# Edge columns of the first graph layer, transposed two chunks at a time and read from half of the array's rows

## The reference, cut to what matters

```
def _rgcn_layer(x, src, dst, edge_type, edge_attr, W, root, bias, nn_w, nn_b):
    edge_w = edge_attr @ nn_w.T + nn_b          # 50000 x 32 by 32 x 256
    msg = relu(x[src] * edge_w)
    out = x @ root + bias
    for r in range(3):
        m = where((edge_type == r)[:, None], msg, 0.0)
        s = segment_sum(m, dst)
        cnt = segment_sum(mask, dst)
        out = out + (s / max(cnt, 1)) @ W[r]
    return out
h = x
for l in range(3):                              # three passes, own W, root, bias; same nn_w, nn_b
    h = _rgcn_layer(h, ..., W[l], root[l], bias[l], nn_w, nn_b)
```

## Time and profile before

| | |
|---|---|
| median of three runs | 4751.31 us |
| span of the profiled execution | 4744.9 us (the page has no other time of it) |
| TensorE matmul busy | 3915.0 us, 83% |
| TensorE weight load busy | 3233.3 us, 68% |
| VectorE busy | 3382.7 us, 71% |
| ScalarE busy | 1791.0 us, 38% |
| GpSimd busy | 3071.7 us, 65% |
| DMA | 643 MB, 136 GB/s on average |

### The profile page before, as it was taken

The page is one execution under the profiler, slowest core; times in us unless marked ns, Lnnn a source line. Parts: engine busy times, 40 slices in busy tenths (PEclk is TensorE's granted clock), DMA queues, the critical chain, the costliest instruction groups (busy, mean ns, idle before and its releaser), DMA issues. The chain is left out here.

```text
span 4744.9 us, 105920 instructions
## 1 busy us (share of the span) xinstructions
PE 3915.0 (83%) x22300; PEld 3233.3 (68%) x22301; DVE 3382.7 (71%) x9318; ACT 1791.0 (38%) x5399; POOL 3071.7 (65%) x3178
## 2 busy tenths in 40 slices
PE   6799997889987889878899566779978778578886
PEld 3477775778776778767777556668866666366664
DVE  7799997667757778677787667874257778756666
ACT  0355553221123333333333100004257667367774
POOL 0266665777756777567775777766777773067774
PEclk9799998999998999989999777888978898778787
DMA  1233334856626445264452687861465444144445
GB/s 47 92 131 131 130 132 130 212 126 158 152 63 202 135 145 154 71 185 146 145 149 78 208 257 214 245 191 54 145 182 120 105 106 125 32 99 109 109 109 100
DMA packets 643665, 643.00 MB, mean 136 GB/s; under 512 B 314342, under 2 KB 549540, under 8 KB 643396
## 3 DMA queue, kind: packets, MB, share of 16 engines
q0 software_dynamic: 145840, 374.54, 27.8%
q1 hardware_dynamic: 443348, 213.36, 17.0%
q10 hardware_dynamic: 54336, 53.65, 3.3%
HBM read 470.09 MB, written 170.26 MB: 135 GB/s over the span
## 5 line engine op out<-in xcount | busy, mean ns | idle before, releaser
L1059 POOL DMA_INDIRECT G<-h_dram,idx x1572 | 1525.8, 971 | 556.8 <-issue 361.6
L1283 PEld LDWEIGHTS ps_a<-hotm,msg 128*128 128x128 f32 x4716 | 686.5, 193 | 196.2 <-DVE arena L1395 67.5
L1283 PE MATMUL ps_a<-hotm,msg 128*128 128x128 f32 x4716 | 730.0, 282 | 88.5 <-DVE arena L1395 87.8
L1271 PE MATMUL ps_e<-nnw,attT 128*128 128x256 f32 x2358 | 738.4, 396 | 76.8 <-DVE prodm L1388 42.4
L1395 DVE TENSOR_TENSOR arena<-ps_a,arena 128x256 f32 x1404 | 586.9, 418 | 218.8 <-issue 94.1
L735 POOL DMA_INDIRECT rec_dram<-rec,pos x392 | 376.7, 961 | 398.6 <-ACT rec L606 307.7
L1059 POOL DMA_INDIRECT G<-feat_dram,idx x420 | 402.4, 958 | 325.5 <-POOLq L241 197.9
L1317 ACT ACTIVATE msg<-prodm 128x256 f32<-128x256 f32 x786 | 327.5, 417 | 677.8 <-DVE prodm L1388 586.1
L749 POOL DMA_INDIRECT rec_dram<-rows,place x392 | 379.8, 969 | 222.1 <-issue 117.4
L1897 POOL DMA_INDIRECT arena<-rel_dram,idx x393 | 385.0, 980 | 128.6 <-issue 86.2
L1271 PEld LDWEIGHTS ps_e<-nnw,attT 128*128 128x128 f32 x2358 | 370.3, 195 | 118.4 <-DVE prodm L1388 56.4
(11 more groups left out here) (365 smaller groups left out, 7691.6 us busy)
## 6 DMA issues: line engine op xcount, KB each, us to landing
gate<-rec_dram SPq DMA_DIRECT2D x126, 384.0 KB
G<-msg_dram SPq DMA_DIRECT2D x300, 128.0 KB, 2.2
msg_dram<-msg ACTq DMA_DIRECT2D x270, 128.0 KB
rel_dram<-stage SPq DMA_DIRECT2D x25, 1040.0 KB
G<-h_dram,idx POOLq DMA_INDIRECT x1572
aT<-edge_attr SPq DMA_DIRECT2D x98, 128.0 KB
msg_dram<-arena ACTq DMA_DIRECT2D x90, 128.0 KB
attT<-attT_dram SPq DMA_DIRECT2D x74, 144.0 KB
```

The source lines that it names most:

```text
L1059: pool.indirect_dma_start(G[:, n % width, :], None, table, bass.IndirectOffsetOnAxis(ap=idx[:, which, n:n + 1], axis=0)).then_inc(sem(f"sw ...
L1271: t.matmul(ps_e[s % BANKS][:], attT[:, s // HU, s % HU, :], nnw[:], start=True, stop=True).then_inc(sem("ew"), 1)
L1283: last = t.matmul(ps_a[s % BANKS][:, h, :], of[:, h * P:(h + 1) * P], hot[:, s, :], start=True, stop=True)
```

## The change

- Layer 0 loads edge rows into `att` with 64 columns per chunk. Column 32 is set to one and columns 33 to 63 to zero once.
- TensorE transposes two chunks, 128 columns, at once; the first chunk lands in rows 0 to 63 and the second in rows 64 to 127 of `ps_t`, and one ScalarE copy of 128 x 128 takes both to `attT[:, s // 2]`. A late turn's thirteenth chunk goes alone.
- The edge matmul takes its weights and its `nnw` from 33 rows: 0 to 32 for the first chunk of a pair, 64 to 96 for the second. `nnw` is in both halves. In layer 0 the edge matmul follows the transpose by two steps in place of one.
- `attT_dram` has 128 partitions in place of 32, and a turn's two pieces are 10 and 8 chunks in place of 9 and 9.
- `begin_rgcn` is gone; the four DMAs of `nnw` stand in the kernel's first block.
- In layer 0 the cast for the first turn comes first, and one memset of the whole `arena` follows.
- Bucket numbers are loaded for 18 chunks at once, once a turn, in the three layers and in the gated one.

```
+HALF = P // 2
+PIECES1 = ((0, HU + 1), (HU + 1, U))
-    attT_d = dram("attT_dram", (A32, NC1, P))
+    attT_d = dram("attT_dram", (P, TURNS1 * HU, P))
...
+                        for lo in (0, HALF):
+                            sp.dma_start(nnw[lo:lo + A32, :], L0_gnn_nn_w).then_inc(sem("nnw_in"), 16)
+                            sp.dma_start(nnw[lo + A32:lo + A32 + 1, :], L0_gnn_nn_b.rearrange("(a d) -> a d", a=1)).then_inc(sem("nnw_in"), 16)
...
-                begin_rgcn(nnw, attT)
...
+        def ends_pair(c):
+            return c and not c.extra and (c[2] % 2 == 1 or c.late and c[2] == FRONT - 1)
+        def pair_size(c):
+            return c[2] % 2 + 1
...
-                        att = sb(pctx, "att", [P, U, A32]) if l == 0 else None
+                        att = sb(pctx, "att", [P, U, HALF]) if l == 0 else None
-                        ps_t = ps(pctx, "ps_t", [A32, 2, P]) if l == 0 else None
+                        ps_t = ps(pctx, "ps_t", [P, P]) if l == 0 else None
...
-                                    sp.dma_start(attT[0:A32, h, 0:count, :], attT_d[:, ds(first, count), :]).then_inc(sem(f"att_in{h}"), 16)
+                                    sp.dma_start(attT[:, pairs, :], attT_d[:, ds(i * HU + lo // 2, -(-hi // 2) - lo // 2), :]).then_inc(
+                                        sem(f"att_in{h}"), 16)
...
-                                for c0, c1, c7 in walk(nc.tensor, TURNS1, 0, 1, 7, seams=(SEAM,), late=True):
+                                for c0, c1, c7 in walk(nc.tensor, TURNS1, 0, 2 if l == 0 else 1, 7, seams=(SEAM,), late=True):
...
-                                    if c0 and not c0.extra and l == 0:
+                                    if ends_pair(c0) and l == 0:
                                         n, i, s = c0
-                                        if s % QU == 0:
-                                            pe.wait_ge(sem(f"att_in{s // QU}"), (i + 1) * 16)
-                                        pe.wait_ge(sem("attT_sb"), upto(earlier(c0, 1)))
-                                        t.transpose(ps_t[:, s % 2, :], att[:, s, :], ident[:]).then_inc(sem("attT"), 1)
+                                        for q in range((s - pair_size(c0)) // QU + 1, s // QU + 1):
+                                            pe.wait_ge(sem(f"att_in{q}"), (i + 1) * 16)
+                                        pe.wait_ge(sem("atts_set"), 1)
+                                        pe.wait_ge(sem("attT_sb"), upto(c0.m - pair_size(c0)))
+                                        t.transpose(ps_t[:], att[:, s - s % 2:s - s % 2 + 2, :].rearrange("p s w -> p (s w)"),
+                                                    ident[:]).then_inc(sem("attT"), pair_size(c0))
...
-                                        t.matmul(ps_e[s % BANKS][:], attT[:, s // HU, s % HU, :], nnw[:], start=True, stop=True).then_inc(sem("ew"), 1)
+                                        rows = slice(s % 2 * HALF, s % 2 * HALF + A32 + 1)
+                                        t.matmul(ps_e[s % BANKS][:], attT[rows, s // 2, :], nnw[rows, :], start=True, stop=True).then_inc(sem("ew"), 1)
...
-                                            nc.scalar.copy(attT[0:A32, s // HU, s % HU, :], ps_t[:, s % 2, :]).then_inc(sem("attT_sb"), 1)
+                                        nc.scalar.copy(attT[:, s // 2, :], ps_t[:]).then_inc(sem("attT_sb"), pair_size(c0))
...
                                 if l == 0:
-                                    half = KD * D // 2
-                                    v.memset(arena[:, 0:half], 0.0).then_inc(sem("zeroed"), 1)
+                                    v.memset(att[:, :, A32:A32 + 1], 1.0)
+                                    v.memset(att[:, :, A32 + 1:HALF], 0.0).then_inc(sem("atts_set"), 1)
                                     dve.wait_ge(sem("meta_in"), 16)
                                     v.tensor_copy(idx[:, 0, 0:U], meta[:, 0:U, 1]).then_inc(sem("columns"), 1)
-                                    v.memset(arena[:, half:KD * D], 0.0).then_inc(sem("zeroed"), 1)
-                                    dve.wait_ge(sem("zeroed"), 2)
...
+                                v.memset(arena[:], 0.0).then_inc(sem("zeroed"), 1)
...
-                                bucket = Buckets(nc, mybir.EngineType.DVE, bmap[0:1, 0, :], KD - 1, 8, part=HU)
+                                bucket = Buckets(nc, mybir.EngineType.DVE, bmap[0:1, 0, :], KD - 1, 8, part=U)
...
-                            bucket = Buckets(nc, mybir.EngineType.DVE, bmap[0:1, 1, :], T - 1, 8, part=HU)
+                            bucket = Buckets(nc, mybir.EngineType.DVE, bmap[0:1, 1, :], T - 1, 8, part=U)
```

More of the change, by code:

```diff
@@ L761, in build @@
         meta2 = arena[:, meta2_at:meta2_at + NC2 * REC2].rearrange("p (n w) -> p n w", n=NC2)
[L764 to L780, removed]
         def empty_pads(sp, empty):
@@ L1304, in _ @@
-                                    if c1 and not c1.extra:
-                                        n, i, s = c1
-                                        if l == 0 and (s % HU == HU - 1 or c1.late and s == FRONT - 1):
-                                            wait_ahead(act, (sem("attT_sb"), upto(c1.m)))
-                                            count = s % HU + 1
-                                            nc.scalar.dma_start(attT_d[:, ds(c1.m - (count - 1), count), :], attT[0:A32, s // HU, 0:count, :]).then_inc(
-                                                sem(f"att_out{s // HU}"), 16)
+                                        act.wait_ge(sem("attT"), upto(c0.m))
@@ new lines, in _ @@
+                                        seam = c0.late and isinstance(i, int) and i == SEAM and s % 2 == 0
+                                        act.wait_ge(sem("ew"), upto(turn_before(c0) + (1 if seam else 0)))
+                                        for h, (lo, hi) in enumerate(PIECES1):
+                                            if s - s % 2 == lo and not (isinstance(i, int) and i == 0):
+                                                act.wait_ge(sem(f"att_out{h}"), i * 16)
+                                        nc.scalar.copy(attT[:, s // 2, :], ps_t[:]).then_inc(sem("attT_sb"), pair_size(c0))
@@ new lines, in _ @@
+                                    if c1 and l == 0:
+                                        n, i, s = c1
+                                        for h, (lo, hi) in enumerate(PIECES1):
+                                            if s == (min(hi, FRONT) if c1.late else hi) - 1:
+                                                wait_ahead(act, (sem("attT_sb"), upto(c1.m)))
+                                                pairs = slice(lo // 2, s // 2 + 1)
+                                                nc.scalar.dma_start(attT_d[:, ds(i * HU + lo // 2, s // 2 + 1 - lo // 2), :], attT[:, pairs, :]).then_inc(
+                                                    sem(f"att_out{h}"), 16)
```

35 lines of the change are left out of this document (17 added, 18 removed).

## The result

The changed kernel takes a median of 5625.98 us over four runs (5605.23 to 5752.77), the kernel before 4750.11 (4744.28 to 4754.04): a ratio of 1.183, 95% interval 1.179 to 1.187. Forecast were 4985 us in a range of 4810 to 5060. The direction was right and the size was not: 876 us were lost, where the sum had 237. The slowest of the four runs had a lower clock (0.774) than the others (0.80), and the ratio goes by the others. The profiled execution has a span of 5603.6 us, 858.7 more than before, and the mean granted clock of TensorE is 0.804.

A forecast was written before the change was run, and what follows sets the result against it. Early turns were taken to wait for gathers, late ones for TensorE and VectorE; afterwards TensorE bounds. Terms +249 - 4 - 6 - 2 = +237 on span 4744.9 gave 4982, by the runs' median 4988, rounded to 4985 us; range 4810 to 5060.

The forecast's parts named there:

- The price of the change of form: Three relational layers: leaving and re-entering 128-row matmuls around each 33-row edge matmul costs TensorE 0.40 us per main chunk.
- The term was +249: Three relational layers: longer early and late turns, 19 + 50 us in layer 0 and 90 in each other layer.
- that TensorE keeps its clock: Three relational layers: turns were summed at unchanged operation times, from a trace with granted clock 0.97 to 1.00; no term.
- rival 4: Three relational layers: 33 rows of 128 could leave TensorE at 1.2 GHz, doubling operations, over +1000 us; chance 0.02.
- One bucket load: Relational and gated layers: loading 18 values once costs nothing extra in the relational layers and saves 4 us in the gated.
- The +58 kept for the range: Late turns of the relational layers: up to 1.3 us more at each turn start if load time goes with count.
- The row at turn start: Layer 1 before the change: VectorE builds one-hots, loads bucket numbers, then sits 1.14 us at turn start.
- Pairs: Layer 0: 393 transposes become 204, saving 0.055 us per main chunk; ScalarE's copies halve in number and hide.
- the end of the mid-turn stall: Late turns of layer 0: TensorE's 0.74 us stall goes, as it may run three chunks ahead, now 4 us.
- Setup stage: Stage from 165.13 to 171.74 us goes, -6.6; its weight DMAs move to kernel start, +0.6; -6 us in all.
- Cast first: Start of layer 0: first gathers start 8 us sooner, but TensorE bounds the turns, so only -2 us.
- Doubled column loads: Layers 1 and 2: loads double from 288 to 576 KB a turn; taken at nothing, bounds 0 and +10 us.

The follow-up runs named there:

- narrow form alone: The kernel before with one edit, its edge matmuls reading rows 0 to 32 of both operands: 5441.51 us, ratio 1.145.
- 64-row run: The kernel before with its edge matmuls reading rows 0 to 63 of both operands: 5110.59 us, ratio 1.077.
- VectorE three times: The kernel before with each product of VectorE computed three times, twice into a tile that nobody reads: 5509.97 us, ratio 1.160.

## Why the prediction was wrong

- **The price of the change of form: right.** 0.39 us per change at full clock, 0.40 taken. The Trainium skill, TensorEngine Tiling (Array Packing), Key Properties, says that a change of mode drains the engine; the traces agree, for rows, and add the price. Turns at full clock, read in the runs with 33 rows (layer 0) and with 64 rows (layer 1), average 25.8 us early and 21.9 late in layer 0, 23.6 and 20.5 in layer 1, against 24.8 (pairs included), 22.2, 23.9 and 21.5. The excess over the earlier trace rows is 11 x 2.7 + 15 x 3.0 in layer 0 and 11 x 2.5 + 15 x 2.9 in each of the others, 217 us. The term was +249.
- **The failed step: that TensorE keeps its clock** while TensorE is the bound. It stood nowhere as a term; it was rival 4, with 0.02. Of the 689 us of the narrow form alone some 217 are its price at full clock, so some 470 are lost by the clock. The argument against rival 4 was the earlier trace rows, eight 64-row operations over in 0.71 us. These are twice the rows, four waves of two side by side, among streams of 128 rows. They say that one excursion does not change the clock at once, not what 18 a turn do. The 64-row run shows how far that was off: with twice the rows the kernel is at 5111, beside the range of the forecast, and not at 5442. Rival 4 also had it as all or nothing, over +1000; it came at 0.58 to 0.85.
- The Trainium skill, TensorE: Matmul & The Clock Gate, Why this matters for your kernels, asks for no long idle gaps between matmul bursts if drops are to be avoided. The traces agree where there is such a gap: TensorE comes out of 4.03 us of idle time at the lower level with the edge matmuls back on 128 rows, and the clock is 0.85 with VectorE three times. But this alone does not explain layer 1 with narrow matmuls, where the profile shows no idle time in ten turns at 0.58 and 0.59. The drained gap, which it counts as busy, is not enough either, since the run with 64 rows has the same one and turns at 1.00. So rows that stand still count too; by what rule is open.
- **One bucket load: wrong**, 49 us where -4 stood (nothing in the layers, -4 in the gated one). "One load instruction serves all nine" was no reason for 18 costing the same. The +58 kept for the range was the right size. The row at turn start stands for every second turn start only; the others had no gap before. With one load the gaps are 3.14 and 0.64 us in turn.
- **Pairs: wrong in sign.** 0.055 us per chunk is true (transposes take 0.11 each), but in late turns TensorE lives on its lead over VectorE's stalls, and the second step of lag took a bank of it. I had put the end of the mid-turn stall into the sum and no price on the lag: 40 us.
- **Setup stage:** 3.3 us, not 6. The stage is gone, but the next operation of VectorE starts at 168.48 after a wait of its own of 3.40 us, against 171.74 in the earlier trace rows. **Cast first:** no gain to be measured, -2 forecast. **Doubled column loads:** right, TensorE waits for them four times, 29.8 us, against 25.9 in the earlier trace rows.
- **Together** the other parts cost 57 us alone and 184 beside the narrow form (5626 less 5442). Why they cost more there is open: longer idle stretches would fit, but taking them back by two loads made the changed kernel 59 us slower.

## What to carry to other kernels

Before you give an operation fewer rows of the array, count the changes of form around it (0.39 us each here), and then ask what share of the array works over the whole loop: a matmul on a quarter of the rows saves nothing in its own time, zeros in the unused rows cost nothing, and without them the whole loop can fall to 1.2 GHz though the profile shows TensorE busy throughout. A term for the granted clock belongs in any sum for a TensorE-bound loop that makes it work less densely, with a chance that is worked out and not waved off by one short stretch. And a step of lag is not free where an engine bridges stalls on its lead.

## What the runs showed of the hardware that I had not expected

- The clock falls under a TensorE that the profile shows busy without a break: 0.59 with 33-row matmuls for a third of the operations (half of the columns) and a gap of 0.39 us per chunk; 0.89 with 64 rows and the same gaps; 0.93 with 65 rows and none; 0.98 with 128. These are means over ten turns of layer 1; with 64 rows two turns are slow and eight at 1.00.
- Adding two full-row matmuls per chunk to it brings the clock from 0.59 to 0.97 and shortens ten turns from 376.9 to 326.2 us, in the fastest of four runs; by the median the kernel as a whole had no gain from it.
- A load of 18 register values leaves VectorE idle for 3.13 to 3.15 and 0.64 us at alternate turn starts; one of nine left 1.14 and nothing, and 0.8 at mid-turn. The loop's body holds two turns; whether its end makes the difference was not tried.
- The gap of a change of form is the same from 33 and from 64 rows, 0.39 us.
